# Weight-row transfers of the last layer moved from ScalarE's queue to SyncE's inside two attentions, with doubled row buffers and a one-slot later use

## The reference, cut to what matters

```python
x = x + attention_i(layernorm(x), context)    # i = 0..3
x = x + ffn_i(layernorm(x))                   # i = 0..3
```

```python
scale = max(|W| over a row) / 127
q = round(W / scale) * scale
y = round8(x_in) @ q.T + x_out @ W.T + b      # x_out: columns whose maximum is over 3
```

## Time and profile before

| | |
|---|---|
| Time, median of 3 runs | 1977.71 us (1975.74 to 1980.68) |
| Profiled execution, its own time | 1977.77 us |
| Span of the profiled execution | 1976.0 us |
| Around the span | 1.8 us |
| PE busy | 1828.1 us, 93% of the span |
| DVE, ACT, POOL busy | 74%, 53%, 42% |
| Granted TensorE clock, mean | 0.975 |
| First and last `nmax` of the two attentions | 606.7 us, 1480.2 us |

### The profile page before, as it was taken

How to read it: one execution, slowest core, us unless ns; L and a number is a source line. 1 busy time by engine, 2 the same in 40 slices (tenths; PEclk the granted TensorE clock), 3 DMA queues, 4 the chain that set the end, 5 groups by cost and what they waited for, 6 DMA issues and landing times.

```text
span 1976.0 us, 29931 instructions
## 1 busy us (share of the span) xinstructions
PE 1828.1 (93%) x10468; PEld 1502.8 (76%) x10468; DVE 1457.8 (74%) x2984; ACT 1046.0 (53%) x2019; POOL 829.6 (42%) x815
## 2 busy tenths in 40 slices
PE   6999999999897999986899999999996999998988
PEld 5888888888776787875687887887875877776755
DVE  6777787777685887774677777767774477787898
ACT  5766666656414544550365555555561177786333
POOL 6554654463453222115334343434225813151762
PEclk9999999999999999997999999999998999999899
DMA  4101101010115989672377868878883100120210
GB/s 161 54 23 54 54 33 54 22 54 22 49 46 101 201 178 194 115 140 79 81 160 152 175 147 175 161 165 154 156 158 114 51 23 22 44 86 1 89 45 22
DMA packets 372115, 188.42 MB, mean 95 GB/s; under 512 B 341632, under 2 KB 351104, under 8 KB 364672
## 3 DMA queue, kind: packets, MB, share of 16 engines
q1 hardware_dynamic: 358144, 165.54, 37.5%
q10 hardware_dynamic: 13824, 20.98, 3.5%
HBM read 97.08 MB, written 5.24 MB: 52 GB/s over the span
## 4 chain that ended last, share of the span: by engine, by line
PE 40%; DVE 15%; ACT 5%; POOL 4%; issue 4%; DMA 3%; ACTq 1%; SPq 1%; POOLq 0%; DVEq 0%
PE ps_t L351 5%; PE ps_s L351 5%; PE ps_t L352 4%; PE ps_t L353 4%; PE ps_s L353 4%; PE ps_s L352 4%; PE ps_o L2147 3%; PE ps_t L2178 3%; DVE l_ab L1587 2%; DVE nmax L1582 2%; PE ps_s L2133 2%; PE ps_o L351 2%; PE ps_o L353 2%; PE ps_o L352 2%; ACT ps_s L1544 2%
## 5 line engine op out<-in xcount | busy, mean ns | idle before, releaser
L1582 DVE TENSOR_REDUCE nmax<-ps_s 128x1 f32<-128x768 f32 x192 | 183.3, 954 | 112.7 <-PE ps_s L353 112.0
L1528 ACT ACTIVATE l_ab<-ps_s,rinv 128x768 f16<-128x768 f32 x192 | 173.0, 901 | 171.1 <-DVE w_int L679 55.5
L1544 ACT ACTIVATE ps_s<-ps_s,nmax 128x768 f32<-128x768 f32 x192 | 167.7, 874 | 167.7 <-DVE nmax L1582 167.1
L351 PE MATMUL ps_s<-l_k_hi,l_q_hi 128*128 128x512 f32 (+3 forms) x512 | 199.8, 390 | 37.4 <-DVE l_ab L1587 34.8
L1587 DVE SCALAR_TENSOR_TENSOR l_ab<-ps_s,rinv,l_ab 128x768 f16<-128x768 f32 x192 | 194.0, 1011 | 22.5 <-ACT l_ab L1528 22.3
L389 POOL TENSOR_TENSOR wo_hi<-raw_big,one 128x512 fp32r<-128x512 f32 (+2 forms) x100 | 102.0, 1020 | 222.8 <-PE ps_t L353 170.7
L352 PE MATMUL ps_s<-l_k_lo,l_q_hi 128*128 128x512 f32 (+3 forms) x512 | 181.4, 354 | 0.0
L353 PE MATMUL ps_s<-l_k_hi,l_q_lo 128*128 128x512 f32 (+3 forms) x512 | 181.0, 354 | 0.0
L351 PE MATMUL ps_o<-l_pt,l_v 128*128 128x256 f16 (+1 forms) x576 | 160.6, 279 | 14.9 <-DMA l_v<-l_vab 8.8
L389 POOL TENSOR_TENSOR wq_hi<-raw_big,one 128x512 fp32r<-128x512 f32 (+1 forms) x100 | 108.4, 1084 | 136.0 <-DMA raw_big<-in_l_wq 85.0
L353 PE MATMUL ps_o<-l_pt,l_v 128*128 128x256 f16 (+1 forms) x576 | 160.0, 278 | 0.0
(11 more groups left out here) (407 smaller groups left out, 5711.6 us busy)
## 6 DMA issues: line engine op xcount, KB each, us to landing
raw_big<-in_l_wq SPq DMA_DIRECT2D x18, 1024.0 KB, 5.2
raw_big<-in_l_wo SPq DMA_DIRECT2D x18, 1024.0 KB, 5.0
w_raw<-in_f_w ACTq DMA_DIRECT2D x32, 256.0 KB, 3.4
raw_big<-in_f_w SPq DMA_DIRECT2D x7, 1024.0 KB, 4.8
raw_kv<-in_l_wkv SPq DMA_DIRECT2D x12, 512.0 KB, 5.8
raw_f<-in_f_w SPq DMA_DIRECT2D x4, 1024.0 KB, 4.8
w_nat<-in_f_w1n ACTq DMA_DIRECT2D x16, 256.0 KB, 3.7
w_nat<-in_f_w2n ACTq DMA_DIRECT2D x16, 256.0 KB, 3.2
```

Source lines behind the costliest of these rows:

```text
L351: pe.matmul(o, a[0], b[0], start=start, stop=False)
L1528: e.activation(sp.ab[:, (k - 1) % 3, 0, :], self.scores_out(k - 1), ACT.Copy, scale=rinv[:, i:i + 1]).then_inc(s_pa, 1)
L1544: e.activation(self.scores_out(k), self.scores_out(k), ACT.Exp, bias=nmax[:, i:i + 1], accum_out=rsum[:, i:i + 1]).then_inc(s_exp, 1)
L1582: e.tensor_reduce(nmax[:, i:i + 1], self.scores_out(k), AX.X, ALU.max, negate=True).then_inc(s_max, 1)
```

## The change

The method `act` of both helpers becomes `sp`, called in SP's list after the transposes of the slot and before its big weight loads. `w_nat` has four buffers and `w_raw` and `w_int` two each. DVE reduces and rounds two slots after the load was issued instead of one, and the store is issued three slots after the load instead of two. The waits of a load are for a tile four (two) before. Nothing is computed differently.

```diff
-            def act(self, e, k):
+            def sp(self, e, k):
                 n = self.step_at(k)
                 if n is not None:
-                    if n >= 2:
-                        e.wait_ge(s_nmax, n - 1)
-                    e.dma_start(w_nat[n % 2][:, :], self.source(n)).then_inc(s_nat[n % 2], 16)
+                    if n >= 4:
+                        e.wait_ge(s_nmax, n - 3)
+                    e.dma_start(w_nat[n % 4][:, :], self.source(n)).then_inc(s_nat[n % 4], 16)
...
             def dve(self, e, k):
-                n = self.step_at(k - 1)
+                n = self.step_at(k - 2)
...
-            def act(self, e, k):
-                p = self.load.get(k - 2)
+            def sp(self, e, k):
+                p = self.load.get(k - 3)
                 if p is not None:
                     e.wait_ge(s_wrnd, p + 1)
-                    e.dma_start(self.target(p), w_int[:, :]).then_inc(s_wout, 16)
+                    e.dma_start(self.target(p), w_int[p % 2][:, :]).then_inc(s_wout[p % 2], 16)
                 p = self.load.get(k)
                 if p is not None:
-                    if p:
-                        e.wait_ge(s_wrnd, p)
-                    e.dma_start(w_raw[:, :], self.source(p)).then_inc(s_wraw, 16)
+                    if p >= 2:
+                        e.wait_ge(s_wrnd, p - 1)
+                    e.dma_start(w_raw[p % 2][:, :], self.source(p)).then_inc(s_wraw[p % 2], 16)
...
-                p = self.load.get(k - 1)
+                p = self.load.get(k - 2)
                 if p is not None:
                     e.wait_ge(s_wmul, p + 1)
-                    if p:
-                        e.wait_ge(s_wout, 16 * p)
-                    e.tensor_scalar(w_int[:, :], w_raw[:, :], MAGIC, -MAGIC, ALU.add, ALU.add).then_inc(s_wrnd, 1)
+                    if p >= 2:
+                        e.wait_ge(s_wout[p % 2], 16 * (p // 2))
+                    e.tensor_scalar(w_int[p % 2][:, :], w_raw[p % 2][:, :], MAGIC, -MAGIC, ALU.add, ALU.add).then_inc(s_wrnd, 1)
...
                 for k in self.slots:
-                    if self.maxima:
-                        self.maxima.act(e, k)
-                    if self.rounding:
-                        self.rounding.act(e, k)
...
                     for kv, b in self.sets.get(k - 1, ()):
                         self.cross_values(e, kv, b)
+                    if self.maxima:
+                        self.maxima.sp(e, k)
+                    if self.rounding:
+                        self.rounding.sp(e, k)
```

More of the change, by code:

```diff
@@ L224, in program @@
         w_rc = at("w_rc", [P, 4], F32, 117.4375)
-        w_nat = [at(f"w_nat{i}", [P, 512], F32, 12 + 2 * i) for i in range(2)]
-        w_raw = at("w_raw", [P, 512], F32, 12)
+        w_nat = [at(f"w_nat{i}", [P, 512], F32, 8 + 2 * i) for i in range(4)]
+        w_raw = [at(f"w_raw{i}", [P, 512], F32, 8 + 2 * i) for i in range(2)]
+        w_int = [at(f"w_int{i}", [P, 512], BF16, 12 + i) for i in range(2)]
         w_row = at("w_row", [P, 512], F32, 14)
-        w_int = at("w_int", [P, 512], BF16, R0 + 89)
         w1_ints = nc.dram_tensor("first_weight_rounded", (P, DK, FFN_H), BF16, kind="Internal").ap()
@@ L293, in program @@
         s_qk = sem("rotated_operand_ready")
-        s_nat = [sem("even_rows_in"), sem("odd_rows_in")]
+        s_nat = [sem(f"rows_in_{i}") for i in range(4)]
         s_nmax = sem("row_maxima")
@@ L298, in program @@
         s_wrow = sem("inverse_scales_row")
-        s_wraw = sem("weight_rows_in")
+        s_wraw = [sem("even_weight_rows_in"), sem("odd_weight_rows_in")]
         s_wmul = sem("weight_rows_scaled")
         s_wrnd = sem("weight_rows_rounded")
-        s_wout = sem("rounded_rows_stored")
+        s_wout = [sem("even_rounded_rows_stored"), sem("odd_rounded_rows_stored")]
         s_wback = [sem("first_weight_rounded_in"), sem("second_weight_rounded_in")]
@@ L607, in dve @@
                     to = q_sw1[:, n:n + 1] if n < 16 else w_am[:, a:a + 1]
-                    e.wait_ge(s_nat[n % 2], 16 * (n // 2 + 1))
-                    e.tensor_reduce(to, w_nat[n % 2][:, :], AX.X, ALU.max, apply_absolute_value=True).then_inc(s_nmax, 1)
+                    e.wait_ge(s_nat[n % 4], 16 * (n // 4 + 1))
+                    e.tensor_reduce(to, w_nat[n % 4][:, :], AX.X, ALU.max, apply_absolute_value=True).then_inc(s_nmax, 1)
                     if n >= 16 and a == 3:
@@ L692, in pool @@
                     if p is not None:
-                        e.wait_ge(s_wraw, 16 * (p + 1))
+                        e.wait_ge(s_wraw[p % 2], 16 * (p // 2 + 1))
                         e.wait_ge(s_tlo, row_ready(self.chunk(p)))
-                        e.tensor_tensor(w_raw[:, :], w_raw[:, :], w_row[:, :], ALU.mult).then_inc(s_wmul, 1)
+                        e.tensor_tensor(w_raw[p % 2][:, :], w_raw[p % 2][:, :], w_row[:, :], ALU.mult).then_inc(s_wmul, 1)
             def pe(self, e, k, take_turn_bank, piece):
@@ L1518, in act @@
                 for k in self.slots:
[L1519 to L1522, removed]
                     if 0 <= k - 1 < self.N:
@@ L1837, in f2_pool @@
             split_all(e, "o", c2.o, c2.g - 4)
-            e.wait_ge(s_wout, 16 * row_rounding.pieces)
+            for stored in s_wout:
+                e.wait_ge(stored, 8 * row_rounding.pieces)
             split_all(e, "f", 1, c2.g - 4)
```

## The result

The changed kernel takes 1954.5 us, median of 4 runs (1953.3 to 1958.6), beside 1979.2 us for four runs of the kernel before on the same chip. The ratio is 0.988, 95% interval 0.9857 to 0.9902. Timed twice more, in other sets of runs, it came to 0.9896 [0.9877, 0.9914] and 0.9892 [0.9875, 0.9909].

What follows compares the result with a forecast made beforehand. PE, 93% busy, was taken as the bound, with 24.6 us of its waits for DVE as the prize. 1977.8 - 6.4 (second layer) - 12 (third layer) + 1.4 (late landing) = 1960.8, so 1961 us, range 1951 to 1973.

Steps and rivals of the forecast that it cites:

- case 1: Whole run: all terms as summed, 1961 us, own range 1952 to 1967; chance 0.62.
- Second layer, -6.4: Row maxima stretch: PE waits 4.4 us less at two group boundaries and 2.0 us less elsewhere; bounds 0 and 8.4.
- Third layer, -12: Rounding stretch: DVE's waits for POOL and ACT go, so PE's 16.2 us of waits shrink by 12; bounds 5 and 16.2.
- the three quarters: Third layer: share of PE's 16.2 us of waits taken as gain, 12 us, since a few lie in the last eighth.
- the low case's sum: Whole run with the third layer's lower bound and two queueing costs: 1977.8 - 4.4 - 9 + 4 = 1968.
- the fall of the granted clock at 1100.9: Third layer: clock falls to 1.2 GHz for 3.4 us after a PE wait, losing 1.7 us; left out of the sum.
- SP's queue, 0: SP takes 96 issues; later transposes cost 0, or about 2 us at each of two boundaries if cover is gone.
- the late landing, +1.4: Row tiles land later behind transposes and 1 MB loads in SP's queue, costing 1.4 us; bounds 0 and 5.
- case 3: One queue makes tiles late, so POOL's multiplication and DVE's rounding stay late at group boundaries: 1969 us; chance 0.16.
- case 4's threshold of 2.0 us an issue: Second layer: SP becomes the bound if a group's 16 new issues exceed 2.0 us each; at 2.7, 1988 us; chance 0.08.
- I count 0: Second layer: a transpose delayed in SP's queue costs nothing, since its result is used some four slots on.
- DVE is covered: Row tiles landing later through SP's queue do not hold DVE, as they get one more slot, about 4 us.

Runs made afterwards that it cites:

- rounding part alone: Kernel before with only the rounding's half: SP issues, two buffers, rounding two slots after the load, store three; 1960.3 us, ratio 0.9909.
- the timed half: Kernel before with only the maxima's half: SP issues, four buffers, reduction two slots after the load; 1972.5 us, ratio 0.9977.
- ACT kernel with the use as before: Changed kernel with ACT issuing, buffers and store kept, but reduction and rounding one slot after the load; 1952.4 us, ratio 0.9877.
- the one with two issues: Changed kernel with each of the 32 maxima loads issued as two halves of 64 partitions; 1967.2 us, ratio 0.9957.

## Why the prediction was right, and what in it was off

**The forecast held**, case 1, 1954.5 us in that case's own range of 1952 to 1967, with a gain of 21 to 24 us where 17 were summed. Three of its four marks are in the profile: ACT's `l_ab` waits for no row tile; DVE's waits for ACT's `l_ab` and for `w_raw` are gone; PE waits 3.9 us for `l_ab` in the rounding stretch, where under 6 was named. The fourth, under 3 us in the maxima stretch, was missed at 4.4.

**Second layer, -6.4.** The two profiles say -11.3, and taken alone they mislead. The kernel with the rounding part alone runs the second layer in the order of before and took 269.1 us where the profile of before has 274.2. With the maxima's part on SP the four profiles have 262.9, 268.0, 263.6 and 269.0. The means are 271.7 and 265.9, 5.8 us apart, and the timed half gave 4.5 (2.0 to 7.1). The term was right within that, and one pair of profiles is not a measurement of a stage to better than 5 us. As PE's idle time, which is what the term summed, the same six profiles give 24.5 and 20.9, so 3.6 us; PE's waits for `l_ab` fell from 8.4 us to 4.2 to 4.8 in the three changed profiles. The rest is busy time. The working was off in two places: at a boundary PE idled 1.99 us, not "at least as long" as DVE's 2.24, and the four remaining waits held 3.7 us, not 2.0.

**Third layer, -12.** Repeated profiles agree here: 518.7 and 518.9 us with the old rounding, 500.4 to 504.1 with the new one on SP. From the windows, PE's idle time fell by 518.7 - 489.89 - (503.1 - 486.07) = 11.8 us, so the term was right for what it counted, though the three quarters in it were a choice (and the low case's sum used 9 us as its lower bound where 5 stood in the working). What came on top is 3.8 us less of PE's busy time. 1.7 us of it is the fall of the granted clock at 1100.9, for which nothing similar is seen after (I had put it in the low end); for the other 2 us I have no cause. The reason given for the term was half wrong: I let the later use take away 11.3 us of DVE's waits for POOL. The ACT kernel with the use as before shows that once the store and the load no longer wait in ACT's list, these waits shrink to 4.6 us and cost nothing that shows.

**SP's queue, 0, and the late landing, +1.4.** The sum of both was measured as nothing: SP or ACT as issuer makes 0.9872 to 0.9896 either way, once nothing late stands in the issuer's list. `w_raw` lands in 3.6 us median against 3.4, and at worst 4.5 against 8.1; `w_nat` in 3.8 against 3.4, and at worst 6.1 against 9.6. The two tiles of the second layer that SP issued 2 to 3 us behind the load of `wo` landed in 6.1 us each; at the same places on ACT's queue it had been 5.6 and 9.6. By the Trainium skill (DMA: Bandwidth & Descriptors, Queues, rings and completion order) each DMA engine takes turns between the queues that have work for it, from which the prediction made its case 3. The trace does not bear that case out: tiles behind a big load land late in either queue, the medians grew by 0.4 us at most, and case 3 fell. By the Trainium skill's other rule (the same page, Rules for kernel authors), spreading over issuing engines saves issue time alone, and the trace agrees in that the issuer as such is worth nothing that shows. What the change would have been worth by that rule alone, next to nothing, was not what came, since the waits in front of the issues held ACT far longer (143.6 us) than the 96 issues did (32 us).

**The step that failed without costing the forecast** is case 4's threshold of 2.0 us an issue. It was the mean room of SP over a group, from a list of 43 us. The room was smaller: in 640 to 800 us SP of the kernel before waited 48.5 us for `l_ab`, 1.5 us for each of 32 issues. Measured, 0.85 us a tile is free and 1.5 us costs some 13 us. Nor is it a matter of the mean alone, for SP's own waits in 640 to 800 us are the same in the changed kernel

```profile
SPq L1389 <- DVE l_ab L1583: 23.2, 17, 3.1
```

and in the one with two issues:

```profile
SPq L1390 <- DVE l_ab L1584: 23.8, 17, 2.9
```

SP stood idle for 23 us in both: it is late in some slots, above all behind the head moves and the load of `wo`, and idle in others. For the transposes "I count 0" held as far as PE goes, which waited for no `l_pt` by name, but ACT, which has to empty the buffer, waited 6.8 us. The larger oversight is in the row tiles. The prediction named their extra slot as cover ("DVE is covered") without a price for its absence; without it the change costs 46 us, about twice its gain. The forecast hung on that slot more than the text saw, since case 3 was weighed as a matter of queueing among packets, while the danger was SP's own order.

**Behind the two layers, +3.1.** The code there is unchanged; the granted clock over it is 0.96 before and 0.95 after, and (1 - 0.96) x 495.8 = 19.8 against (1 - 0.95) x 498.9 = 24.9 us of lost clock, each good to 2.5. Read in short windows over the stage and summed, it is 19.5 us before and 23.6, 23.7 and 23.6 in the three profiles of the changed kernel, 4 us more, which is enough for it. Other profiles have 496.2 to 499.1 with the third layer fast, 494.9 to 497.1 with it slow. Why the clock falls in other places there was not settled.

## What to carry to other kernels

A wait in front of a DMA issue is a wait of the engine: before moving the issue to another engine, ask how late the thing is that it waits for, since one more buffer or a store one slot later can end the wait where it stands (here that gave the whole gain, with ACT as issuer). Moving an issue to a queue that is reached late in a slot costs the use a slot; give it that slot first, or lose 2%. Judge the room of an issuing engine at its fullest slots, not by its mean alone: 0.85 us a tile was free, 1.5 us was not.

## What the runs showed of the hardware that was not expected

The same load of 256 KB takes 0.33 us to issue on ACT and 0.57 to 1.4 us (median near 0.9) on SP between transposes, while two of half the size take 0.6 us each in the median and 1.5 us as a pair. The second transpose of 128 x 768 behind the load of `wo` takes 3.5 to 4.1 us to issue in place of 1.5, at two places each in the profiles before and after, and the first lands after 6.9 to 10.6 us where the median is 4.2 to 4.5. And the second layer's stage, with the same order of instructions, came out at 274.2 and 269.1 us in two profiles, by 2.7 us of PE's busy time and 2.4 us of its idle time.
